# A windowed-attention block on one core: row-tiled turns, centring folded into the MLP's weights, Newton steps for the last inverse deviation

## The reference

```python
xw = windows(x)                                   # 256 windows, 64 tokens, 32 channels
h = _ln(xw, ln1_g, ln1_b)
q, k, v = split_heads(h @ qkv_w.T + qkv_b)        # 4 heads of 8
attn = softmax(q * hd ** -0.5 @ k.T + bias[rpb])  # 64 x 64 for each window and head
o = merge_heads(attn @ v)
xw = xw + o @ proj_w.T + proj_b
h = _ln(xw, ln2_g, ln2_b)                         # (t - mean) * rsqrt(var + eps) * g + b
h = gelu(h @ fc1_w.T + fc1_b)                     # 32 -> 128, exact gelu
xw = xw + h @ fc2_w.T + fc2_b                     # 128 -> 32
```

## Time and profile before

| | us |
|---|---|
| median of 3 runs (lowest, highest) | 167.74 (167.59, 167.76) |
| the profiled execution | 167.38 |
| its span, first to last instruction | 165.6 |
| TensorE busy | 152.5 |
| ScalarE busy | 126.8 |
| VectorE busy | 120.5 |
| GpSimd busy | 91.5 |

### The profile page before, as it was taken

The page is one execution under the profiler, slowest core; times in us unless marked ns, Lnnn a source line. Parts: engine busy times, 40 slices in busy tenths (PEclk is TensorE's granted clock), DMA queues, the critical chain, the costliest instruction groups (busy, mean ns, idle before and its releaser), DMA issues.

```text
span 165.6 us, 6356 instructions
## 1 busy us (share of the span) xinstructions
PE 152.5 (92%) x2688; PEld 85.8 (52%) x2688; DVE 120.5 (73%) x222; ACT 126.8 (77%) x185; POOL 91.5 (55%) x103
## 2 busy tenths in 40 slices
PE   7979799999999999999999999999999988887972
PEld 7635455674566547656755765476576454111111
DVE  3667995969896987889698969878896942453332
ACT  4445967678797889788887979797876469798990
POOL 7600769547685958586766759585868543003000
PEclk9999999999999999999999999999999999999999
DMA  3780000000000000000000000000000000013233
GB/s 78 201 255 6 0 2 4 4 0 4 2 8 0 4 0 4 6 2 4 4 4 0 4 4 2 4 4 0 4 6 0 4 0 4 0 63 117 77 127 127
DMA packets 3245, 4.71 MB, mean 28 GB/s; under 512 B 946, under 2 KB 1298, under 8 KB 3218
## 3 DMA queue, kind: packets, MB, share of 16 engines
q1 hardware_dynamic: 2840, 4.23, 7.5%
q0 software_dynamic: 256, 0.07, 0.4%
q10 hardware_dynamic: 122, 0.01, 0.1%
HBM read 2.21 MB, written 2.10 MB: 26 GB/s over the span
## 4 chain that ended last, share of the span: by engine, by line
PE 72%; ACT 11%; DVE 8%; issue 7%; ACTq 1%; DVEq 0%
PE ps L722 13%; PE ps L740 10%; PE ps L704 10%; PE ps L632 10%; PE ps L747 8%; ACT pt L270 6%; PE ps L679 5%; PE ps L656 4%; PE ps L785 3%; PE ps L638 3%; PE ps L614 2%; DVE s_sb L499 2%; PE ps L799 2%; ACT hid L359 2%; DVE mx L509 1%
## 5 line engine op out<-in xcount | busy, mean ns | idle before, releaser
L219 POOL TENSOR_TENSOR s_sb<-s_sb,mx 128x512 f32<-128x512 f32 x64 | 66.4, 1043 | 43.2 <-DVE mx L509 43.2
L499 DVE TENSOR_TENSOR s_sb<-ps,bias_t 128x512 f32<-128x512 f32 x64 | 43.7, 683 | 8.3 <-PE ps L704 8.3
L509 DVE TENSOR_REDUCE mx<-s_sb 128x8 f32<-128x512 f32 x64 | 43.8, 685 | 1.9
L722 PEld LDWEIGHTS ps<-ident,s_sb 128*128 128x128 f32 x256 | 27.4, 140 | 20.8 <-issue 12.5
L722 PE MATMUL ps<-ident,s_sb 128*128 128x128 f32 x256 | 35.4, 280 | 0.6 <-POOL s_sb L219 0.6
L270 ACT ACTIVATE pt<-ps 128x1024 f32<-128x1024 f32 x24 | 24.4, 1018 | 10.1 <-issue 7.2
L740 PEld LDWEIGHTS ps<-pt,v_blk 128*32 128x32 f32 x1024 | 15.2, 110 | 9.8 <-ACT pt L270 9.3
L740 PE MATMUL ps<-pt,v_blk 128*32 128x64 f32 x1024 | 17.6, 220 | 1.7 <-ACT pt L270 1.7
L704 PE MATMUL ps<-k_m,q_sb 32*64 32x256 f32 x512 | 17.9, 387 | 0.3 <-DVE s_sb L499 0.2
L359 ACT ACTIVATE hid<-ps,fb 128x1024 f32<-128x1024 f32 (+2 forms) x16 | 16.9, 1110 | 1.7 <-PE ps L785 1.7
L632 PE MATMUL ps<-h,wqk 64*64 64x512 f32 x64 | 17.0, 613 | 0.9 <-DVE h L517 0.9
(11 more groups left out here) (95 smaller groups left out, 187.4 us busy)
## 6 DMA issues: line engine op xcount, KB each, us to landing
x_sb<-in_x_dram SPq DMA_DIRECT2D x8, 256.0 KB, 5.1
out_dram<-y_sb SPq DMA_DIRECT2D x7, 256.0 KB, 2.0
out_dram<-y_sb SPq DMA_DIRECT2D x2, 128.0 KB, 1.8
raw_b<-in_L_conv_rpb_dram POOLq DMA_DIRECT2D x8, 8.0 KB, 2.8
f_nat<-in_L_conv_fc_w_dram SPq DMA_DIRECT2D x2, 16.0 KB
w_nat<-in_L_conv_qkv_w_dram ACTq DMA_DIRECT2D x1, 12.0 KB
p_nat<-in_L_conv_proj_w_dram SPq DMA_DIRECT2D x1, 4.0 KB
vec_r<-in_L_conv_ln_g_dram ACTq DMA_DIRECT2D x1, 0.1 KB
```

What stands on the lines that cost most here:

```text
L219: pool.tensor_tensor(tile, tile, mx[:, n % 4, :].unsqueeze(2).to_broadcast([128, 2 * NH, NT]), ALU.subtract).then_inc(shifted, 1)
L499: dve.tensor_tensor(s_sb[:, n % NSB, :, :, :].rearrange("p a h m -> p a (h m)"), S_PS[g].rearrange("p (a k) -> p a k", a=2), bias_t[:, :, ...
L509: dve.reduce_max(mx[:, n % 4, :], s_sb[:, n % NSB, :, :, :].rearrange("p a h m -> p (a h) m"), AX.X)\
L722: ins = pe.transpose(T_PS[u][:, 128 * i:128 * (i + 1)], s_sb[:, n % NSB, pr, 2 * hp:2 * hp + 2, :].rearrange("p h m -> p (h m)"), ident[:, :])
```

## The change

- `turn` goes in two row tiles: each unit's rows 0 to 63 and 64 to 127 (two windows) are transposed apart, 16 transposes of 64 rows and 64 streamed columns for a round in place of eight, rows 0 to 63 into bank 4 and the others into bank 5. So both units of a round share both banks; a turn waits for both units' subtraction and for the exp of all of the round before; exp always takes 1024 columns; `pt` and its readers follow the new order, and add_bias waits by whole rounds.
- q, k: `crossed` for `straight`; project, center2: `straight` for `crossed`; the columns of wv and the output groups of down follow.
- The second centring is put into the weights: f1_s = cent_m x (g2 * fc1), by one more matmul in the set-up. norm2 multiplies x1_sb; keep2 goes, square2 reads Y_PS.
- The last chunk's variance is taken with tokens on partitions (variance2_last, 128x16), inverted on VectorE by a bit trick and three Newton steps (inv_std2_last), copied to 128x512 and turned back by TensorE (spread_inv_std2); VectorE does norm2_last. ScalarE's second and third table loads go.
- gelu: bank sets repeat in threes, always two activations of 1024 columns, `hid` has four buffers. The order of up, down and the last norm after the loop is written out.

```diff
@@ exp_round
-                if r == 0:
-                    for u in range(2):
-                        act.activation(pt[:, n % 8 + u, :, :, :].rearrange("p a k n -> p (a k n)"), T_PS[u], ACT.Exp)\
-                           .then_inc(expd, 1)
-                else:
-                    act.activation(pt[:, n % 8:n % 8 + 2, :, :, :].rearrange("p u a k n -> p (u a k n)"),
-                                   ps[:, 4:6, :].rearrange("p u n -> p (u n)"), ACT.Exp).then_inc(expd, 2)
+                act.activation(pt[:, n % 8 // 2, :, :, :, :, :].rearrange("p b u a k n -> p (b u a k n)"),
+                               ps[:, 4:6, :].rearrange("p b n -> p (b n)"), ACT.Exp).then_inc(expd, 2)
@@ turn
-                for u in range(2):
-                    n = unit(c, r, u)
-                    pe.wait_ge(shifted, n + 1)
-                    if n >= 2:
-                        pe.wait_ge(expd, n - 1)
+                n = unit(c, r, 0)
+                pe.wait_ge(shifted, n + 2)
+                if n >= 2:
+                    pe.wait_ge(expd, n)
...
+                            for ab in range(2):
+                                rows = slice(NT * ab, NT * (ab + 1))
+                                ins = pe.transpose(T_PS[ab][:, NT * i:NT * (i + 1)],
+                                                   s_sb[rows, (n + u) % NSB, pr, 2 * hp:2 * hp + 2, :]
+                                                   .rearrange("p h m -> p (h m)"),
+                                                   ident[rows, rows], tile_position=(NT * ab, 0))
@@ set_up_late_biases (TensorE)
+                pe.wait_ge(setup_b, 4)
+                pe.matmul(Y_PS[:, 128:256], cent_m[:, :], f1_g[:, :], start=True, stop=True).then_inc(setup_t, 1)
@@ norm2, square2
-                pool.tensor_tensor(h2_sb[:, p, :], h2_sb[:, p, :], rstd2[:, :], ALU.mult).then_inc(h2_ready, 1)
+                pool.tensor_tensor(h2_sb[:, p, :], x1_sb[:, p, :], rstd2[:, :], ALU.mult).then_inc(h2_ready, 1)
-                act.activation(sq2[:, :], h2_sb[:, p, :], ACT.Square).then_inc(squared2, 1)
+                act.activation(sq2[:, :], Y_PS, ACT.Square).then_inc(squared2, 1)
@@ VectorE, last inverse deviation (each step waits for the one before)
+            def inv_std2_last():
+                dve.wait_ge(var2_ready, NCH)
+                dve.tensor_scalar(var_t[:, :], Y_PS[:, 0:4 * G], 1e-5, None, ALU.add).then_inc(newton, 1)
...
+                for step in range(3):
+                    dve.wait_ge(newton, 3 + 3 * step)
+                    dve.tensor_tensor(part_t[:, :], inv_t[:, :], inv_t[:, :], ALU.mult).then_inc(newton, 1)
...
+                dve.tensor_copy(inv_x[:, :, :, :].rearrange("p t g c -> p (t g) c"),
+                                inv_t[:, :].unsqueeze(2).to_broadcast([128, 4 * G, C])).then_inc(rstd2_ready, 1)
+            def norm2_last():
+                dve.wait_ge(spread, 1)
+                dve.wait_ge(h2_ready, NCH - 1)
+                dve.tensor_tensor(h2_sb[:, NCH - 1, :], x1_sb[:, NCH - 1, :], Y_PS, ALU.mult).then_inc(h2_ready, 1)
@@ TensorE after the loop
+            def variance2_last():
+                for t in range(4):
+                    ins = pe.matmul(Y_PS[:, G * t:G * (t + 1)], sq2[:, 128 * t:128 * (t + 1)], mean_m[:, 0:128:C],
+                                    start=True, stop=True)
+            def spread_inv_std2():
+                pe.wait_ge(rstd2_ready, NCH)
+                for t in range(4):
+                    ins = pe.matmul(Y_PS[:, 128 * t:128 * (t + 1)], inv_x[:, t, :, :].rearrange("p g c -> p (g c)"),
+                                    ident[:, :], start=True, stop=True)
...
-            down(1, y_bank(1), slice(0, TC))
-            for c in range(2, NCH - 1):
-                up(c + 1)
-                down(c, y_bank(c), slice(0, TC))
+            up(3)
+            wait_variance2(NCH - 1)
+            variance2_last()
+            down(1, y_bank(1), slice(0, TC))
+            up(4)
+            spread_inv_std2()
+            up(5)
+            down(2, y_bank(2), slice(0, TC))
+            down(3, y_bank(3), slice(0, TC))
+            up(6)
+            down(4, y_bank(4), slice(0, TC))
+            up(7)
+            down(5, y_bank(5), slice(0, TC))
+            down(6, y_bank(6), slice(0, TC))
```

More of the change, by code:

```diff
@@ L127, in swin_block_kernel @@
         hidden_ready, gelu_ready, down_ready, y_ready = sem("hidden_ready"), sem("gelu_ready"), sem("down_ready"), sem("y_ready")
[L128 removed]
+        stored, newton, spread = sem("stored"), sem("newton"), sem("spread")
         block = ctx.enter_context(nc.Block())
@@ L231, in _ @@
                         subtract_max(c, 0, g)
-                if there(c - 2):
+                if there(c - 2) and c - 2 < NCH - 1:
                     norm2(c - 2)
@@ L368, in _ @@
                     blank_values(1)
-                if p == NCH:
-                    act.preload_act_table_set("natural_log_exp_and_others")
-                if there(p - 1):
+                if there(p - 1) and p < NCH:
                     log_var2(p - 1)
-                if p >= NCH - 1:
+                if p == NCH - 1:
                     inv_std2(p - 1)
@@ L488, in set_up_late_biases @@
             def set_up_late_biases():
-                dve.wait_ge(setup_t, 4)
+                dve.wait_ge(setup_t, 5)
+                dve.tensor_copy(f1_s[:, :], Y_PS[:, 128:256])
                 dve.tensor_scalar(fb1[:, :], Y_PS[:, 1:2], fc1_bc[:, :], None, ALU.add)
@@ L663, in make_k @@
             def make_k(f):
-                straight(X_PS, wqk[:, 1, :], h1[:, f % 2, :, :].rearrange("p w n -> p (w n)")).then_inc(k_ready, 1)
+                crossed(X_PS, wqk[:, 1, :], h1[:, f % 2, :, :].rearrange("p w n -> p (w n)")).then_inc(k_ready, 1)
             def wait_q(f):
@@ L670, in make_q @@
             def make_q(f):
-                straight(S_PS[0 if f else 1], wqk[:, 0, :], h1[:, f % 2, :, :].rearrange("p w n -> p (w n)"))\
+                crossed(S_PS[0 if f else 1], wqk[:, 0, :], h1[:, f % 2, :, :].rearrange("p w n -> p (w n)"))\
                     .then_inc(q_ready, 1)
@@ L746, in attend @@
                     for g in range(G):
-                        ins = pe.matmul(OD_PS[t][C * g:C * (g + 1), 256:512], ones_h[:, hp, :],
-                                        pt[:, (4 * t + g) % 8, :, hp, :], start=(hp == 0), stop=(hp == 1),
+                        ins = pe.matmul(OD_PS[t][C * g:C * (g + 1), 256:512].rearrange("p (a b n) -> p a b n", a=2, b=2),
+                                        ones_h[:, hp, :],
+                                        pt[:, (4 * t + g) // 2, :, g % 2, :, hp, :].rearrange("p b a n -> p a b n"), start=(hp == 0), stop=(hp == 1),
                                         tile_position=(0, C * g))
@@ L755, in project @@
             def project(p):
-                crossed(Y_PS, wp[:, :, :].rearrange("p g c -> p (g c)"), att).then_inc(projected, 1)
+                straight(Y_PS, wp[:, :, :].rearrange("p g c -> p (g c)"), att).then_inc(projected, 1)
             def wait_center2(p):
@@ L761, in center2 @@
             def center2(p):
-                crossed(Y_PS, cent_m, x1_sb[:, p, :]).then_inc(centered2, 1)
+                straight(Y_PS, cent_m, x1_sb[:, p, :]).then_inc(centered2, 1)
             def wait_variance2(p):
@@ L818, in _ @@
             set_up_late_biases()
-            for c in range(NCH + 2):
+            for c in range(NCH + 1):
                 f, p = c + 1, c - 1
```

93 lines of the change are left out of this document (55 added, 38 removed).

## The result

| | before | after |
|---|---|---|
| median of 4 runs, us (range) | 167.67 (167.27 to 167.76) | 163.59 (163.33 to 163.87) |
| profiled execution, its span | 167.38, 165.6 | 163.51, 161.7 |
| ratio after to before | | 0.9762, 95% interval 0.9738 to 0.9785 |

A forecast was written before the change was run, and what follows sets the result against it. TensorE, busy 92% of the span, was taken as the bound. Head +0.24, six periods -2.58 and tail -1.63 make -3.97 from 167.38, 163.4; plus 0.36 to the median, 163.7 us. Own range 162.3 to 165.3, with A 162.3 to 166.5.

The forecast's parts named there:

- The length of a turn: TensorE's transposes in two row tiles: pairs 0.058 us apart, 0.61 us a turn against 1.02.
- tiles don't overlap at all: Upper bound for a turn on TensorE: 16 x 54 ns and 0.15 us to the next group give 1.02 us.
- The waits: Loop: exp(c,0) stays at 8.07; turn(c,1) needs all of it and starts at 9.15 us instead of 9.00.
- Hidden by the wait for q: Loop: GpSimd's subtraction releasing turn(c,2) ends at 14.0, out of sight because score(c+1,0) waits for q.
- The period: One loop period, walked: 14.80 us instead of 15.22, put at 0.43 less; six periods -2.58 us.
- The head: Set-up to score(1,0): one more matmul +0.40 us, turn(0,2) gives back 0.16, so +0.24.
- Up to gelu(0): Tail from score(7,0): gelu(0) at 18.6 instead of 20.06 us, -1.46, from keep2's removal and shorter turns.
- The gelu stretch: First to last gelu: 22.5 us instead of 22.67, -0.17; TensorE bounds it, waiting for VectorE's chain ahead of spread.
- A: Rival, turns: load and stream of a pair don't overlap, a turn is 0.9 us; 166.2 us; chance 0.14.
- C: Rival, turns: tiles' loads one behind the other and slow, a turn of 1.9 us; some 190 us; chance 0.04.
- D: Rival, tail: loop as forecast but the chain of small ops takes 4.9 us; +1.5, 165.2 us; chance 0.08.
- B: Rival, turns: tiles don't overlap or each pair costs 108 ns, a turn stays 1.02; 168.2 us; chance 0.12.

The follow-up runs named there:

- waits_only: Kernel before with the new waits and one 1024-column exp in round 0, transposes still 128x128: 171.49 us, ratio 1.0227, periods of 15.62.
- turns_only: Kernel before with the row-tiled turns alone (turn, exp, pt, attend, add_bias's wait): 165.55 us, ratio 0.9876.
- old_turns: Changed kernel with the turns of before (128x128 transposes, two exp halves in round 0, waits by unit): 166.62 us, ratio 0.9945.
- pool_first: Changed kernel with GpSimd's subtract_max(c, 1, 1) ahead of mask_keys: 164.36 us, ratio 0.9782, periods of 14.87.
- exp2_late: Changed kernel with pool_first's order and ScalarE's inv_std2(p-1) moved behind exp(c,0): 163.57 us, ratio 0.9733, periods of 14.65.
- newton_none: Changed kernel without the three Newton steps (nine small VectorE ops left out): 162.76 us, ratio 0.9728.
- newton_double: Changed kernel with six Newton steps instead of three: fastest of four runs 165.62 us, profiled execution 169.34.
- serial_tiles: Changed kernel with a turn's 16 transposes reordered, all eight of row tile 0 first, then row tile 1: 169.47 us, ratio 1.0109.
- all_three: Changed kernel with f1's centring matmul moved behind variance1(1), exp2_late's order and another TensorE order after the loop: 162.88 us, ratio 0.9707.
- best: Changed kernel with f1's centring matmul moved later, exp2_late's order and six blank matmuls in TensorE's chunk 0 waits: 162.24 us, ratio 0.9671.

## Why the prediction was right

- **The length of a turn.** Forecast 0.61 us, measured 0.64. A pair of transposes takes 62 ns and was put at 58 from make_v's row. The bound "tiles don't overlap at all" was too low: a tile alone goes at 62 and not at 54 ns. By the Trainium skill (TensorE: Matmul & The Clock Gate, LDWEIGHTS (loading the stationary operand)) a load of 128 columns takes 107 ns, which would have made a turn 1.0, an estimate from that figure. This trace disagrees for transposes: a tile's follow each other at 62 ns with new weights each, and the first waits 272-223 = 49 ns for its load.
- **The waits.** exp(c,0) at 8.07 was exact, turn(c,1) at 9.19 for 9.15. That the new waits alone cost 0.40 a period (waits_only) and not 0.15 doesn't contradict the sum, in which the saved 0.4 us of turn(c,1) and turn(c,2) stands against it, but it had one of two places. Turn(c,2) was forecast at 13.94 and started at 14.18, released by GpSimd. "Hidden by the wait for q" was right only because the turns are short, and by 0.03 us: of the 0.25 us for which q_sb was to hold score(c+1,0), that is what is left.
- **The period.** 14.80 forecast, 14.85 measured: turn(c,1) was 0.04 late and longer, so exp(c,1) started at 10.02 for 9.91, attend(c,0) at 11.09 for 11.02 and copy_q at 14.11 for 14.05. The saving is 0.37 a period for 0.43, which was rounded up from 15.22-14.80. turns_only and old_turns show that the whole 0.37 is the turns', pool_first that q, exp2_late that ScalarE's chain set the rest.
- **The head.** Score(0,0) at 14.40 for 14.45, score(1,0) at 27.87 for 27.85: score(0,0) came 0.32 us later and not 0.40, and 0.06 and not 0.16 came back in the first period. The fall of the clock behind the new wait in the head, 0.7 us in some executions, was not foreseen.
- **Up to gelu(0).** 18.65 for 18.60. The reason given, keep2 ahead of the last find_max, is half of it: turns_only shows that it also stood ahead of square2.
- **The gelu stretch.** 22.15 for 22.5. Each of the small ops took 0.21 and not 0.24 us, so spread began 31.0 us after score(7,0) (147.95-116.95) instead of 31.5 by the walk, and TensorE's idle ahead of it was 0.97 and not 1.5; newton_none and newton_double show the chain on the path. Behind spread TensorE waits only 0.33 and 0.38 us up to its last group, so there it is the bound as forecast; for the whole stretch this is not shown.
- **The sum.** That 163.59 is so close to 163.7 is in part luck. The six periods saved 2.24 us where 2.58 were forecast, and the gelu stretch 0.52 where 0.17 were: the two misses, a third of a microsecond each, cancel. The 0.36 us from the profiled execution to the median, taken from before, was 0.08 in after.
- **The range.** Its bounds don't add up as written: +0.8, +0.2 and +1.5, and -0.7, -0.2 and -0.9, give 161.9 to 166.2 around 163.7, not 162.3 to 165.3. The measured time is well inside both.
- **Rivals.** A, C and D are out by the length of the turn and of the chain. B is nearly what serial_tiles makes of the kernel, where it was priced at 168.2 us. The median is 169.5, with two of four runs at a clock of 0.986; the profiled execution is 168.8. Its periods are 0.28 us longer than before's and not 0.15, by the second place of the waits, and its first period is 0.5 longer.

## What to carry to other kernels

When the engine that is busy 99% of a loop is made faster, walk one period with the other engines' fixed starts: here TensorE's busy time fell by 1.11 us a period and 0.37 came out, and a walk of the new period led to a reordering on two engines with idle time that gave 0.2 more. Row tiles of short transposes paid here only with the instructions alternating between the tiles, since the coarser waits that they bring cost more than the rest saved. When a change lengthens TensorE's waits near the start, compare the granted clock of several runs; blank matmuls in these waits are worth a try. And add the misses of a forecast up by stretch: a right total can hide two that cancel.

## What was not expected of the hardware

- Transposes of 64 rows and 64 columns in a row tile follow each other at 62 ns, whether the other tile works beside it or not; with the tiles alternating a pair takes those 62 ns, and with one tile's eight ahead of the other's the second tile starts only behind the fifth (serial_tiles).
- The granted clock fell to half behind 2.84 us without a matmul in the tail (newton_double), and in some executions in the head around an idle of 1.2 us, which in others left it up; 0.97 us of idle ahead of spread did not bring it down in after's four runs.
- TensorE stops now and then within a group for 0.3 to 0.7 us where the program has no wait (after, pool_first, all_three, best).
- Small dependent VectorE ops on 128x16 take 0.17 us and follow each other at 0.21, whatever the operation (shift, multiply, fused multiply); the copy that spreads 128x16 to 128x512 takes 0.43.
